# Cross-attention on one core: context phase in matmuls of 256 columns, and the scores' weights moved by 64 bytes

## What is computed

```python
Q = (img_embed @ Wq).reshape(B, -1, H, D).transpose(0, 2, 1, 3)      # img_embed (8, 256, 256)
K = (sent_embed @ Wk).reshape(B, -1, H, D).transpose(0, 2, 1, 3)     # sent_embed (8, 256, 192)
V = (sent_embed @ Wv).reshape(B, -1, H, D).transpose(0, 2, 1, 3)
score = jnp.einsum('bhqd,bhkd->bhqk', Q, K) / math.sqrt(D)
score = jnp.where(mask, score, -jnp.inf)
attn = jax.nn.softmax(score, axis=-1)
ctx = jnp.einsum('bhqk,bhkd->bqhd', attn, V).reshape(B, -1, H * D)
out = ctx @ Wo + img_embed
mu = jnp.mean(out, axis=-1, keepdims=True)
var = jnp.var(out, axis=-1, keepdims=True)
return (out - mu) * jax.lax.rsqrt(var + EPS) * gamma + beta
```

## Time and profile before

| | us |
|---|---|
| median of three runs | 319.12 |
| the profiled execution | 319.14 |
| its span, first to last instruction | 317.3 |
| TensorE busy | 309.8 |
| VectorE busy | 253.0 |
| ScalarE busy | 221.9 |
| GpSimd busy | 181.2 |

### The profile page before, as it was taken

How to read it: one execution, slowest core, us unless ns; L and a number is a source line. 1 busy time by engine, 2 the same in 40 slices (tenths; PEclk the granted TensorE clock), 3 DMA queues, 4 the chain that set the end, 5 groups by cost and what they waited for, 6 DMA issues and landing times.

```text
span 317.3 us, 7411 instructions
## 1 busy us (share of the span) xinstructions
PE 309.8 (98%) x2264; PEld 290.7 (92%) x2264; DVE 253.0 (80%) x721; ACT 221.9 (70%) x601; POOL 181.2 (57%) x183
## 2 busy tenths in 40 slices
PE   8899999999999999999999999999999999999993
PEld 7898888999999999999999999999999999999982
DVE  0466778777999879987998889987998889975686
ACT  2446677768867787678777797678767887777640
POOL 1123476457864587558855586558755686457312
PEclk9999999999999999999999999999999999999999
DMA  7995443464344553484446444364356435440101
GB/s 257 365 409 219 136 155 130 141 211 136 99 146 169 189 166 121 140 243 136 132 128 198 156 154 158 131 215 150 115 190 180 169 101 186 144 138 20 35 0 66
DMA packets 46910, 50.26 MB, mean 158 GB/s; under 512 B 3504, under 2 KB 37040, under 8 KB 46896
## 3 DMA queue, kind: packets, MB, share of 16 engines
q1 hardware_dynamic: 46608, 49.56, 47.2%
q10 hardware_dynamic: 288, 0.52, 0.6%
HBM read 32.24 MB, written 17.83 MB: 158 GB/s over the span
## 4 chain that ended last, share of the span: by engine, by line
PE 93%; DMA 2%; DVE 2%; ACT 1%; SPq 1%; issue 0%; POOLq 0%; POOL 0%; DVEq 0%
PE score_bank L320 25%; PE out_bank L320 19%; PE gL_bank L320 14%; PE tL_bank L320 13%; PE tU_bank L320 9%; PE gU_bank L320 7%; DMA wq_raw<-in_wqT 2%; PE spare_bank L354 1%; PE tL_bank L354 1%; PE spare_bank L320 1%; PE tL_bank L336 1%; PE tU_bank L336 1%; PE out_bank L360 1%; PE tU_bank L360 1%; DVE tU L827 1%; PE out_bank L336 0%
## 5 line engine op out<-in xcount | busy, mean ns | idle before, releaser
L1003 POOL TENSOR_TENSOR probs<-probs,inv_sum 128x512 f32<-128x512 f32 x64 | 66.6, 1041 | 85.5 <-DVE inv_sum L790 84.9
L601 ACT ACTIVATE probs<-neg_scores,neg_max 128x256 f32<-128x256 f32 x128 | 64.2, 503 | 35.5 <-DVE neg_max L779 35.4
L1026 POOL TENSOR_TENSOR pT_lo<-pT_raw,pT_hi 128x512 fp32r<-128x512 f32 x60 | 76.5, 1297 | 8.6 <-ACT pT_hi L558 8.6
L779 DVE CUSTOM_DVE_ANT_0 neg_scores<-score_bank,mask_bias 128x256 f32<-128x256 f32 x128 | 49.1, 420 | 6.5 <-PE score_bank L320 4.0
L800 DVE STREAM_TRANSPOSE squares<-probs 128x512 f32<-128x512 f32 x60 | 42.3, 706 | 0.5 <-DMA scratch<-squares 0.2
L558 ACT ACTIVATE tL_hi<-tL_bank 128x512 fp32r<-128x512 f32 x31 | 18.5, 598 | 31.5 <-PE tL_bank L320 31.5
L320 PE MATMUL score_bank<-ctxT_hi,gU 128*128 128x256 f32 x128 | 36.5, 285 | 0.0
L727 DVE TENSOR_TENSOR tL_lo<-tL_bank,tL_hi 128x512 fp32r<-128x512 f32 x31 | 21.4, 689 | 18.8 <-ACT tL_hi L558 18.8
L320 PE MATMUL score_bank<-ctxT_hi,gL_lo 128*128 128x256 f32 x128 | 36.2, 283 | 0.0
L320 PE MATMUL score_bank<-ctxT_hi,gL_hi 128*128 128x256 f32 x128 | 36.2, 283 | 0.0
L320 PE MATMUL score_bank<-ctxT_lo,gL_hi 128*128 128x256 f32 x128 | 36.2, 283 | 0.0
(11 more groups left out here) (167 smaller groups left out, 946.8 us busy)
## 6 DMA issues: line engine op xcount, KB each, us to landing
scratch<-squares SPq DMA_DIRECT2D x30, 512.0 KB, 2.7
pT_raw<-scratch SPq DMA_DIRECT2D x120, 128.0 KB, 3.1
xT_raw<-in_xT SPq DMA_DIRECT2D x8, 256.0 KB, 4.5
ctxT_raw<-in_ctxT SPq DMA_DIRECT2D x8, 256.0 KB, 4.7
wo_raw<-in_wo SPq DMA_DIRECT2D x4, 512.0 KB, 13.7
x_res<-in_x SPq DMA_DIRECT2D x8, 256.0 KB, 3.2
out<-y_out SPq DMA_DIRECT2D x7, 256.0 KB, 2.8
wq_raw<-in_wqT SPq DMA_DIRECT2D x3, 512.0 KB, 7.6
```

The costliest lines, as they stand in the source:

```text
L601: nc.scalar.activation(probs[j % 2][:, n, :], neg_scores[:, n, :], ACT.Exp, bias=neg_max[:, n:n + 1], scale=-1.0, accum_out=row_sum[:, n:n ...
L779: nc.vector.tensor_tensor_reduce(out=neg_scores[:, n, :], in0=score_bank[hh][:, q, :], in1=mask_bias[:], scale=-SCALE, scalar=3.0e38, op0= ...
L1003: nc.gpsimd.tensor_tensor(probs[j % 2][:, rows, :], probs[j % 2][:, rows, :], inv, ALU.mult) \
L1026: nc.gpsimd.tensor_tensor(pT_lo[j % 2][:, k].rearrange("p hh (q i r) -> p (hh q) i r", q=QT, i=ROWS), pT_raw[j % 2][:, k].rearrange("p i n ...
```

## The change

And the context phase gives each of its products as two matmuls of 256 columns, one for each head, in place of one of 512 columns: 20 matmuls a step. Only the first matmul into a bank carries the start flag.

```diff
         ctxU = sb("ctxU", [P, KT, 2 * UP], F32R)
+        gL_hi = sb("gL_hi", [P, 2, S], F32R)
+        gL_lo = sb("gL_lo", [P, 2, S], F32R)
+        gU = sb("gU", [P, 2, S], F32R)
         tL_hi = sb("tL_hi", [P, 2, S], F32R)
...
         eps_col = sb("eps_col", [P, QT])
         power_col = sb("power_col", [P, QT])
 
-        gL_hi = sb("gL_hi", [P, 2, S], F32R)
-        gL_lo = sb("gL_lo", [P, 2, S], F32R)
-        gU = sb("gU", [P, 2, S], F32R)
...
+                def halves(into, stationary, moving, first=False, last=False):
+
+                    for hh in range(2):
+                        ins = split_products(into[:, hh, :], [(stationary, moving[:, hh, :])],
+                                             first=first and hh == 0, last=last, shared=True)
+                    return ins
...
-                split_products(tL[:], [(part[:, k, :], hi[:, k]) for k in range(KT) for part in (ctxL_hi, ctxL_lo)],
-                               last=False)
+                for k in range(KT):
+                    halves(tL, ctxL_hi[:, k, :], hi[:, k], first=k == 0)
+                    halves(tL, ctxL_lo[:, k, :], hi[:, k])
...
-                split_products(tU[:], [(ctxU[:, k, :], hi[:, k]) for k in range(KT)], last=False)
+                for k in range(KT):
+                    halves(tU, ctxU[:, k, :], hi[:, k], first=k == 0)
...
-                    lower = split_products(tL[:], [(ctxL_hi[:, k, :], lo[:, k])], first=False, last=end)
+                    lower = halves(tL, ctxL_hi[:, k, :], lo[:, k], last=end)
                     if end:
                         lower.then_inc(t_product, 1)
-                    upper = split_products(tU[:], [(ctxU[:, k, :], lo[:, k])], first=False, last=end)
+                    upper = halves(tU, ctxU[:, k, :], lo[:, k], last=end)
```

More of the change, by code:

```diff
@@ L433, in context_products @@
                     pe.wait_ge(pT_split, 2 * t + 2)
[L434 to L438, removed]
+                    for k in range(KT):
+                        upper = halves(tU, ctxU[:, k, :], lo[:, k], last=k == KT - 1)
@@ L439, in context_products @@
+                    upper.then_inc(t_product, 1)
+                    for k in range(KT):
+                        halves(tL, ctxL_hi[:, k, :], hi[:, k], first=k == 0)
+                        halves(tL, ctxL_lo[:, k, :], hi[:, k])
+                        lower = halves(tL, ctxL_hi[:, k, :], lo[:, k], last=k == KT - 1)
+                    lower.then_inc(t_product, 1)
                     return
-                split_products(tL[:], [(part[:, k, :], hi[:, k]) for k in range(KT) for part in (ctxL_hi, ctxL_lo)],
-                               last=False)
+                for k in range(KT):
+                    halves(tL, ctxL_hi[:, k, :], hi[:, k], first=k == 0)
+                    halves(tL, ctxL_lo[:, k, :], hi[:, k])
```

## The result

| | us |
|---|---|
| kernel before, median of four runs beside it | 319.16 |
| changed kernel, median of four runs | 324.87 (324.56 to 325.08) |
| ratio | 1.0178 (95% interval 1.0163 to 1.0192) |
| profiled execution, changed kernel | 324.79, span 323.0 |

The account below looks back on a forecast made before the run. TensorE, busy without a gap, was taken as the bound, so only the distance between matmul starts counts. 319.14 + 0.16 + 0.06 + 5.0 + 0.3 = 324.6 us; range 314.4 to 325.4, likeliest case 323.8 to 325.4.

Parts of the forecast that it names:

- up to the first score of step 4: Steps 0 to 3 cost +0.16 us, the first context phase +0.06 us, both slow behind plain f32 matmuls.
- 27 steps: Steady stretch: 76 matmuls a step at 117.7 ns, 8.945 us instead of 8.760, together +5.0 us.
- from the first score of step 31 to the end of the span: Tail: small gains and losses of scores, outputs and four context phases, together +0.3 us.
- first context phase: Behind the fold's f32 matmuls, 20 matmuls at the slow beat: 2.46 us instead of 2.40, +0.06 us.
- The slow beat: 117.7 ns between starts of 256-column matmuls with weights and stream on opposite sides; predicted to hold in every steady step.
- fast beat: 113.3 ns between starts of those same matmuls; seen only behind even pairs or 512-column matmuls, both absent from changed steps.
- even pairs: Weights and stream on the same side of the two small columns: 120 ns a matmul; opposite sides are called odd.
- Rival B: The fast beat holds in all steps once set: 8.611 us a step, 314.7 us in all; chance 0.21.
- room of gL_lo: At a batch's end under Rival B: 0.46 us before TensorE needs gL_lo, 0.27 us left, so no stall.
- The split: Context phase as 20 matmuls of 256 columns: -14 ns a step at the fast beat, +74 ns at the slow.
- C: Beat changes with the phase, some groups fast and others slow: 317 to 321 us; chance 0.12.
- D: Moving the tensors does nothing, scores stay at 120 ns, context gains 14 ns a step: 318.7 us; chance 0.03.

Follow-up runs that it names:

- e6: Changed kernel with the first head's two gL_lo matmuls last among its scores and eight unused even matmuls once after step 4: 324.2 us, ratio 1.0157.
- e9: e6 with TensorE's upper output matmuls moved behind the context phase: 325.1 us, ratio 1.0182.
- e10: e6 with VectorE's normalising of a finished batch moved one step later, behind tU_lo: 316.78 us, ratio 0.9922.
- e12: e10 with the scores back in their old order, gL_lo needed by the fifth matmul: 324.44 us, ratio 1.0159.
- e3: Changed kernel plus 20 unused even matmuls once at the end of step 4: three executions at 325.78 to 325.97 us, one at 318.25 us.
- e2: Kernel before with only the context phase split into 256-column matmuls, gL_hi, gL_lo and gU not moved: 319.23 us, ratio 1.0007.
- e1: Kernel before with only gL_hi, gL_lo and gU moved, context phase left at 10 matmuls of 512 columns: 322.95 us, ratio 1.0121.
- e5: Changed kernel with the first head's two gL_lo matmuls behind its eight other score matmuls, nothing added: 324.77 us, ratio 1.0174.
- e7: e6 with four even matmuls in place of eight: 325.35 us, ratio 1.0192.

## Why the prediction was right

It said 324.6 us (its terms add up to 324.66); 324.87 was measured. Its terms against the traces:

| term | predicted | measured |
|---|---|---|
| up to the first score of step 4 (51.18, now 51.44) | +0.16 + 0.06 | +0.26 |
| 27 steps (236.52, now 241.68) | +5.0 | +5.16 |
| from the first score of step 31 to the end of the span (317.34 - 287.70, now 322.96 - 293.12) | +0.3 | +0.2 |

From the profiled execution before (319.14) that makes 324.76; the profiled execution after took 324.79. The last 36 outputs of the tail, for which I had counted nothing, take 0.09 us less (4.51 us before, 4.42 now). The first two rows, in the timeline of the changed kernel (answers the earlier trace rows):

```profile
34.10 0.39 PE L320 MATMUL score_bank<-ctxT_hi,gU 128*128 128x256 f32 x1
...
36.57 0.28 PE L320 MATMUL gU_bank<-xT_hi,A_hi 128*128 128x256 f32 x1
...
48.98 0.50 PE L320 MATMUL tL_bank<-pT_hi,ctxL_hi 128*128 128x256 f32 x2
...
51.44 0.28 PE L320 MATMUL score_bank<-ctxT_hi,gU 128*128 128x256 f32 x1
```

Scores of step 2: 2.47 us (predicted 2.50 - 0.04); first context phase: 2.46 us (predicted 2.46).

**The slow beat.** Read from four short runs of 5 to 16 intervals as 117.7 ns, it was 117.8 over the steady stretch: 241.68 / 27 = 8.951 us for 76, where 8.945 was predicted. That difference, 27 x 0.006 = 0.16 us, is the miss of the second row.

**What sets the fast beat.** Right in the outcome, wrong in the list. I named even pairs and 512-column matmuls. Even pairs can do it: eight of them in e6, e9, e10 and e12, twenty in e3, the scores of step 5 in e2 (from step 6 on the phase ahead of them is fast already). The 512-column phase of e1 never did, in 27 steps and the tail, so it alone doesn't explain; what does is open. And the list is too short: step 0 of e5 is fast behind the fold, where I had every odd run slow. That it did not happen in the changed kernel, where steps 0 to 3 and the first context phase behind the fold are slow, was likely by the rows and not certain: of 44 sets of such scores behind the fold, in eleven traces, that one is fast.

**Rival B.** Its price was right to 0.002 us a step: 8.611 predicted, 8.613 in e10. Its condition, that nothing later disturbs the fast beat, failed twice. The room of gL_lo at a batch's end was mis-sized. I took it from the earlier trace rows as 0.46 us, to the start of the matmul. What has to be in time is the weight load, and step 9 is tighter than the step of the earlier trace rows. VectorE's gL_lo and the load that needs it in step 9 of the kernel before:

```profile
94.39 0.69 DVE L727 TENSOR_TENSOR gL_lo<-gL_bank,gL_hi 128x512 fp32r<-128x512 f32 x1
```

```profile
95.34 0.19 PEld L320 LDWEIGHTS score_bank<-ctxT_hi,gL_lo 128*128 128x128 f32 x1
```

95.34 - 95.08 = 0.26 us, and a load follows VectorE by 0.05 us at the least (97.70 to 97.75 in e3), so 0.21 us were there to spend; my own sum spent 0.19, and in e3 the load came 0.03 us late. The rest held but for the count: a stall under 0.1 us, which handed the beat over to slow, once and not seven times, since the slow beat gives the room back. The second wait, for tU_lo, I hadn't looked for at all; both follow from VectorE's normalising and statistics, which make it late in one step of four.

**Rivals C and D.** C needs groups of one phase at 276 and of another at 279 ns; in the changed kernel all are at 279. D is refuted by the scores, which went from 283 to 279 ns. The Trainium skill (SBUF — State Buffer, Who interferes with whom) gives TensorE independent read ports for the stream and for the weights. By that alone a place could not matter; e1, which differs from the kernel before in a place alone, takes 3.8 us more, and the measurement decides.

**The split.** I bounded its price by -14 and +74 ns a step, reading the phase before as 2.28 us; to the nanosecond its starts give 2.287. At the fast beat the split phase takes 2.267 us (e2), 20 ns less; at the slow one 2.356 us, where the phase of 512-column matmuls takes 2.289 (e1), 67 ns more. The Trainium skill (Perfetto Trace Analysis, Matmuls) says that larger matmuls are more efficient than smaller ones, when possible. For 512 against 256 columns the trace agrees at the slow beat and not at the fast one.

## What to carry to other kernels

Where TensorE never waits, read the distance between starts, not the length of records, and ask what stands ahead of a run of matmuls as well as what is in it: the same instructions can have two paces, and a local saving (2.3 ns on each score) can take away what kept the rest at the better one. Before counting on a state that must not be disturbed, list every wait of the engine with its room, from the end of the producer to the weight load, in the tightest step and not in a typical one; a delay of 0.03 us, next to nothing by itself, cost 0.34 us in each later step here. Moving work on the engine that feeds it (e10) beat moving work on TensorE itself (e9), since an in-order engine turns a later result into a later everything.

## What was not expected of the hardware

- Two paces of the same float32r matmuls (256 columns, weights and stream 64 bytes apart modulo 128), 113.3 and 117.8 ns at the same granted clock of 1.00, each held for as long as nothing disturbs it: 26 steps in e10, 27 in the changed kernel.
- Eight even matmuls (0.95 us) switched to the fast one in each of four traces (e6, e9, e10, e12), four didn't (e7). Twenty can fail: in e2 the even scores of step 4 are followed by slow queries, those of step 5 by fast ones.
- A late load ended the fast pace in e3, e9 and e12 (in e6 it is late by too little to be seen), but one did the opposite. In e9 the scores of step 13 start 0.18 us before their second matmul, a wait of some 0.07 us, and what follows is fast for four steps:

```profile
132.34 0.35 PE L320 MATMUL score_bank<-ctxT_hi,gU 128*128 128x256 f32 x1
132.52 0.28 PE L320 MATMUL score_bank<-ctxT_lo,gU 128*128 128x256 f32 x1
```
